# Layer 0's down projection as three rounded products in place of one fp32 product

## The chip, the cores and the metric

The kernel runs on one core of one Trainium2 chip. Times are device microseconds (us) of one execution. A difference of 0.2% (about 1.6 us) is what a measurement of this kernel can tell from no change.

## What is computed

A model of two layers on 1,024 tokens of width 256. Each layer is attention and a feed-forward part (FFN), both with modulated layer norms. The change touches the FFN of layer 0 alone:

```python
h = silu(x @ w_gate) * (x @ w_up)        # [1024, 1024]
g = h.reshape(..., 256, 4)               # quads of neighbouring columns
_, idx = top_k(abs(g), 2)                # the two largest of each four stay
h_sparse = where(kept, g, 0)
x = x + gb * (h_sparse @ w_down)         # [1024, 1024] @ [1024, 256]
```

## The kernel before, in words

Each engine has its own instruction list, written by hand; engines meet only at semaphores. The four parts (`attention0`, `ffn0`, `attention1`, `ffn1`) follow each other with a barrier between them.

`ffn0` works in 8 units: `u = 2 * c + half`, with `c` one of four chunks of 256 tokens and `half` one of two halves of the 1,024 hidden columns. A unit holds `[128, 4, 256]` numbers, 128 quads on the partitions, the four members `e` of a quad side by side, 256 tokens in each.

- **TensorE** runs, for each unit, `wide(u, wg, ...)` (gate product), `down(u - 2)` (down product of the unit two before), `wide(u, wu, ...)` (up product). The exceptions: units 0 and 1 have no down product, the last unit has none between gate and up. After the last up product come `down(5)`, the modulation rows and columns of layer 1 (`mod_rows`, `mod_columns`), `down(6)` and `down(7)`. After units 1 and 3 four transposes (`turn_x`) bring in the next chunk.
- The gate and up products are already split: `product` adds three rounded products (high times high, high times low, low times high) of operands that were split ahead into a rounded value of type `float32r` and the remainder. The down product is one plain fp32 matmul for each `e` and each of two tiles of 128 tokens, and stands in the profile as two matmul records each.
- **ScalarE** takes `silu` of the gate product, then `magnitude` (absolute values of the unit's rows).
- **VectorE** makes `multiply(u)` (into `h[u % 2]`), then `sparsify(u)`: three comparisons, two sums, two further sums (`wins`), and four selections that set what is not kept to zero in `h[u % 2]`. In odd units `add` brings a finished chunk into `x` and `stats` takes its statistics.
- **GpSimd** scales the rows of `w_down` by the gate of layer 0 (8 instructions of 128x256, in place in `staging`), and later makes the low halves of `x`'s turned rows for chunks 2 and 3.

What orders them around the down product: `down(u)` waits for each of the four selections (`sparse`) and, at u = 0, for the eight scaled pieces of `w_down` (`wd_ready`). `multiply(u)` waits for the up product, and for `down(u - 2)`, since it writes the buffer that this one reads.

## Time and profile before

| what | value |
|---|---|
| median of 3 runs | 776.95 us (776.91 to 776.99) |
| span of the profiled execution, first to last instruction | 776.7 us |
| median less span (what lies around the span) | about 0.25 us |
| TensorE busy, whole span | 721.5 us, 93% |
| VectorE busy, whole span | 556.8 us, 72% |
| ScalarE busy, whole span | 447.5 us, 58% |
| GpSimd busy, whole span | 372.5 us, 48% |
| `ffn0`, first matmul to the last `add` | 444.5 to about 531 us |

The profile is one execution; it gives no separate total for itself beside the span. Its engines are called PE (TensorE), DVE (VectorE), ACT (ScalarE) and POOL (GpSimd). Matmuls overlap, so the distance between two starts says what one costs, and not its length. Names are those of the program without buffer numbers: `staging` holds `w_down`, `ff_h` the unit's rows, `ff_y` the down product's sum.

### The profile page before, as it was taken

The numbers are of one execution on the slowest core, as the hardware profiler recorded it, in microseconds if no ns is written. First come the engines' busy times: TensorE is split into PE (matmuls) and PEld (weight loads), VectorE is DVE, ScalarE is ACT, GpSimd is POOL, SyncE is SP. The second block draws the span as 40 slices with busy tenths as digits, with TensorE's granted clock in tenths as the row PEclk, the third lists the DMA queues.
The fourth block names the chain that finished last, engine by engine and source line by source line (L and its number), as shares of the span: only waits on it lengthen the run. The fifth ranks groups of instructions, "written<-read, shape, count | busy, mean of one in ns | idle before, by whom it ended". The sixth has DMA issues, their size and how long they took to land. (4 is left out here: it accounts for less than half of the span.)

```text
span 776.7 us, 12379 instructions
## 1 busy us (share of the span) xinstructions
PE 721.5 (93%) x4376; PEld 620.7 (80%) x4376; DVE 556.8 (72%) x1263; ACT 447.5 (58%) x924; POOL 372.5 (48%) x403
## 2 busy tenths in 40 slices
PE   6979989999999999999999799999979999789997
PEld 4858878888888888888888689997768778577787
DVE  4656786678766787767776788776579788566666
ACT  2756656667566676666655343322578776546432
POOL 2685556635766357653451330002756545205773
PEclk8999999999999999999999999999999999999999
DMA  7000000000000000004000040004100000000001
GB/s 250 14 8 8 8 22 15 14 2 14 22 15 8 8 15 14 14 8 170 7 8 8 9 128 1 1 1 126 39 0 2 1 1 1 0 4 0 1 1 55
DMA packets 19115, 19.85 MB, mean 26 GB/s; under 512 B 2158, under 2 KB 17006, under 8 KB 19054
## 3 DMA queue, kind: packets, MB, share of 16 engines
q1 hardware_dynamic: 17934, 18.40, 7.3%
q8 instruction: 35, 0.57, 0.3%
q10 hardware_dynamic: 1120, 0.66, 0.3%
q14 instruction: 26, 0.21, 0.1%
HBM read 18.01 MB, written 1.05 MB: 25 GB/s over the span
## 5 line engine op out<-in xcount | busy, mean ns | idle before, releaser
L633 ACT ACTIVATE at_probs<-at_probs,at_negmax 128x128 f32<-128x128 f32 (+7 forms) x128 | 99.6, 778 | 31.8 <-DVE at_negmax L736 29.7
L935 POOL TENSOR_TENSOR at_swapped<-at_swapped,at_sin 128x512 f32<-128x512 f32 x40 | 52.1, 1302 | 136.0 <-ACT at_swapped L611 136.0
L736 DVE CUSTOM_DVE_ANT_0 at_probs<-at_scores,causal 128x128 f32<-128x128 f32 (+7 forms) x128 | 96.1, 751 | 16.8 <-PE at_scores L59 16.2
L524 PE MATMUL at_turn<-ident_sb,at_probs 128*128 128x128 f32 x576 | 85.0, 274 | 13.2 <-DVE at_full_T_lo L752 11.1
L524 PEld LDWEIGHTS at_turn<-ident_sb,at_probs 128*128 128x128 f32 x576 | 66.5, 140 | 21.8 <-issue 8.4
L626 ACT ACTIVATE at_edge_T_hi<-at_turn 128x128 fp32r<-128x128 f32 (+3 forms) x128 | 55.5, 434 | 33.2 <-PE at_turn L524 32.8
L57 PE MATMUL at_scores<-at_kT_hi,room 128*128 128x512 f32 (+1 forms) x192 | 66.4, 346 | 3.4 <-DVE at_negmax L736 3.4
L626 ACT ACTIVATE at_full_T_hi<-at_turn 128x512 fp32r<-128x512 f32 x64 | 38.3, 598 | 49.5 <-PE at_turn L524 47.4
L58 PE MATMUL at_scores<-at_kT_lo,room 128*128 128x512 f32 (+1 forms) x192 | 66.7, 347 | 0.0
L59 PE MATMUL at_scores<-at_kT_hi,room 128*128 128x512 f32 (+1 forms) x192 | 66.3, 345 | 0.0
L752 DVE TENSOR_TENSOR at_edge_T_lo<-at_turn,at_edge_T_hi 128x128 fp32r<-128x128 f32 (+3 forms) x128 | 61.3, 479 | 1.1 <-ACT at_edge_T_hi L626 0.8
L939 POOL TENSOR_TENSOR at_plain<-at_plain,at_swapped 128x512 f32<-128x512 f32 x40 | 51.8, 1296 | 5.7
L766 DVE SCALAR_TENSOR_TENSOR x<-at_proj,at_rinv,x 128x256 f32<-128x256 f32 x122 | 52.9, 475 | 0.1
L757 DVE TENSOR_TENSOR at_att_lo<-at_att,at_att_hi 128x512 fp32r<-128x512 f32 x32 | 22.2, 692 | 38.7 <-ACT at_att_hi L640 38.7
L752 DVE TENSOR_TENSOR at_full_T_lo<-at_turn,at_full_T_hi 128x512 fp32r<-128x512 f32 x64 | 44.1, 689 | 6.7 <-ACT at_full_T_hi L626 5.0
L57 PE MATMUL at_proj<-at_wo_hi,at_att_hi 128*128 128x256 f32 x142 | 45.2, 318 | 3.4 <-DVE x L766 1.9
L726 DVE TENSOR_TENSOR at_plain<-at_scores,at_cos 128x512 f32<-128x512 f32 x30 | 20.7, 692 | 32.4 <-ACT at_swapped L611 32.4
L57 PEld LDWEIGHTS at_scores<-at_kT_hi,room 128*128 128x128 f32 x192 | 36.2, 188 | 9.5 <-issue 2.6
L2124 POOL TENSOR_TENSOR ff_fed_lo<-ff_mid,ff_fed_hi 128x512 fp32r<-128x512 f32 x16 | 20.7, 1294 | 47.0 <-ACT ff_fed_hi L1954 47.0
L944 POOL TENSOR_TENSOR room<-at_plain,room 128x512 fp32r<-128x512 f32 x32 | 41.3, 1292 | 2.7
L57 PE MATMUL at_att<-at_edge_T_hi,at_v 128*128 128x512 f32 (+3 forms) x128 | 42.1, 329 | 0.0
L59 PE MATMUL at_att<-at_edge_T_hi,at_v 128*128 128x512 f32 (+3 forms) x128 | 41.4, 323 | 0.0
(405 smaller groups left out, 2292.3 us busy)
## 6 DMA issues: line engine op xcount, KB each, us to landing
at_wq_in<-L_attn_Wqkv SPq DMA_DIRECT2D x16, 128.0 KB, 2.2
at_wo_in<-L_attn_Wo SPq DMA_DIRECT2D x16, 128.0 KB, 2.0
staging<-L_ffn_routed_w SPq DMA_DIRECT2D x7, 256.0 KB, 4.8
ff_wmod<-L_wmod SPq DMA_DIRECT2D x1, 1536.0 KB, 6.2
at_wmod<-L_wmod SPq DMA_DIRECT2D x1, 1024.0 KB, 8.6
staging<-L_ffn_w_gate SPq DMA_DIRECT2D x1, 1024.0 KB, 5.2
staging<-L_ffn_w_up SPq DMA_DIRECT2D x1, 1024.0 KB, 7.3
staging<-L_ffn_w_down SPq DMA_DIRECT2D x1, 1024.0 KB, 9.7
```

Source lines behind the costliest of these rows:

```text
L57: pe.matmul(out, left.hi, right.hi, start=start, stop=False)
L58: pe.matmul(out, left.hi, right.lo, start=False, stop=False)
L59: return pe.matmul(out, left.lo, right.hi, start=False, stop=stop)
L524: mm = pe.transpose(p_turn[t % 2][:, b - b0, :], probs[:, s % 4, b * P:(b + 1) * P], m.ident[:, :])
L626: act.activation(turned_columns(c, b0, b1, i % 4).hi, p_turn[t % 2][:, 0:b1 - b0, :], ACT.Copy)\
L633: act.activation(row, row, ACT.Exp, scale=-1.0, bias=negmax[:, unit % 4:unit % 4 + 1], accum_out=rowsum[:, unit // NT % 2, i:i + 1])\
L736: dve.tensor_tensor_reduce(out=probs[:, s % 4, 0:width], in0=p_scores[s % 2][:, 0:width], in1=m.causal[:, S - width:], scale=-1.0, scalar= ...
L752: dve.tensor_tensor(out.lo, p_turn[t % 2][:, 0:b1 - b0, :], as_f32(out.hi), ALU.subtract).then_inc(turn_lo, 1)
L766: ins = dve.scalar_tensor_tensor(out=rows, in0=bank[:, t * DM:(t + 1) * DM], scalar=rinv[:, head % 2, 2 * j + t:2 * j + t + 1], in1=rows, ...
L935: turning = pool.tensor_tensor(swapped[:, r % 2, :], swapped[:, r % 2, :], sin[:, cols], ALU.mult)
L939: chain.step(pool.tensor_tensor(turned, turned, swapped[:, r % 2, :], ALU.add))
L944: pool.tensor_tensor(out.lo[:, cols], turned, as_f32(out.hi[:, cols]), ALU.subtract).then_inc(rope_done, 1)
```

## The change

The rows of `w_down` and the kept rows of each unit are split into high and low halves, and `down` calls `product` on them.

- `w_down`: after the eight scalings GpSimd makes eight high halves (`tensor_scalar`, 128x256) and then eight low halves (`tensor_tensor`, 128x256, in place in `staging`). `wd_ready` now counts the low halves.
- Kept rows of units 0 to 6: ScalarE copies `h[u % 2]` to `kept_h[u % 2].hi` (`kept_high(u)`, 128x1024), and GpSimd subtracts (`kept_low(u)`, 128x1024). `down(u)` waits for `kept_lo`, once for the whole unit. `kept_high(u - 1)` stands on ScalarE between `silu(u)` and `magnitude(u)`.
- Unit 7: high halves on ScalarE, one for each `e`, after the reads of the modulation rows; low halves on VectorE, one for each `e`, after `sparsify(7)`.
- `multiply(u)` waits for `kept_low(u - 2)` where it waited for `down(u - 2)`.
- The low halves of `x`'s turned rows for chunks 2 and 3 now stand on GpSimd between `kept_low(0)` and `kept_low(1)`, and between `kept_low(2)` and `kept_low(3)`.

```diff
@@ -1013,11 +1013,13 @@
         wg, wu = m.w_gate, pair("wu", [P, KD, I0])
         wu_in = m.staging[:, 2048:4096].rearrange("p (k n) -> p k n", k=KD)
         wd_in = m.staging[:, 4096:6144]
-        wd = wd_in.rearrange("p (c d) -> p c d", d=DM)
+        wd_lo = nc.alloc_sbuf_tensor_at("ff0_wd_lo", [P, I0 // P, DM], F32R, offset=m.staging_at + 4096 * 4)
+        wd = Split(buf("wd_hi", [P, I0 // P, DM], F32R)[:], wd_lo[:, :, :])
         xn = buf("xn", [P, NT, DM])
         h32 = [buf(f"h32{n}", [P, KD, TOKENS]) for n in range(2)]
         sg, absh = buf("sg", [P, 4, TOKENS]), buf("absh", [P, 4, TOKENS])
         h = [buf(f"h{n}", [P, 4, TOKENS]) for n in range(2)]
+        kept_h = [pair(f"kept_h{n}", [P, 4, TOKENS]) for n in range(2)]
         cx, cy, cz = (buf(n, [P, 2, TOKENS], BF16) for n in ("cx", "cy", "cz"))
         sums = buf("sums", [P, 4, TOKENS], BF16)
         wins = buf("wins", [P, 4, TOKENS], BF16)
@@ -1030,6 +1032,7 @@
         gate_mm, up_mm, silu_done, mul_done, abs_done = (sem(n) for n in ("gate_mm", "up_mm", "silu_done", "mul_done", "abs_done"))
         compared, summed, won, sparse = (sem(n) for n in ("compared", "summed", "won", "sparse"))
         down_mm, added = sem("down_mm"), sem("added")
+        kept_hi, kept_lo, last_lo, wd_gated, wd_hi = (sem(n) for n in ("kept_hi", "kept_lo", "last_lo", "wd_gated", "wd_hi"))
         wmod_in, c_wide, mod_mm, mod_read = (sem(n) for n in ("wmod_in", "c_wide", "mod_mm", "mod_read"))
         mods = [p_x[n][:, :, :].rearrange("p k t -> p (k t)") for n in range(2)]
 
@@ -1079,11 +1082,14 @@
                         pe.wait_ge(wd_ready, I0 // P)
                     if c and not half:
                         pe.wait_ge(added, 2 * c)
+                    if u < UNITS - 1:
+                        pe.wait_ge(kept_lo, u + 1)
                     for e in range(4):
-                        pe.wait_ge(sparse, 4 * u + e + 1)
+                        if u == UNITS - 1:
+                            pe.wait_ge(last_lo, e + 1)
                         for n in range(2):
-                            mm = pe.matmul(p_y[n][:, 0:DM], h[u % 2][:, e, n * P:(n + 1) * P], wd[:, 2 * e + half, :],
-                                           start=(half == 0 and e == 0), stop=(half == 1 and e == 3))
+                            mm = product(pe, p_y[n][:, 0:DM], kept_h[u % 2][:, e, n * P:(n + 1) * P], wd[:, 2 * e + half, :],
+                                         half == 0 and e == 0, half == 1 and e == 3)
                     mm.then_inc(down_mm, 1)
 
                 def mod_rows(n):
@@ -1157,6 +1163,18 @@
                         act.wait_ge(compared, 3 * u)
                     act.activation(absh[:, :, :], h[u % 2][:, :, :], ACT.Abs).then_inc(abs_done, 1)
 
+                def kept_high(u):
+
+                    if u >= 2:
+                        act.wait_ge(down_mm, u - 1)
+                    if u < UNITS - 1:
+                        act.wait_ge(sparse, 4 * u + 4)
+                        act.activation(kept_h[u % 2].hi, h[u % 2][:, :, :], ACT.Copy).then_inc(kept_hi, 1)
+                    else:
+                        for e in range(4):
+                            act.wait_ge(sparse, 4 * u + e + 1)
+                            act.activation(kept_h[u % 2].hi[:, e, :], h[u % 2][:, e, :], ACT.Copy).then_inc(kept_hi, 1)
+
                 def read_rows():
                     act.wait_ge(mod_mm, 1)
                     act.activation(m.mod_row[:, 0, :], mods[0][:, 0:DM], ACT.Copy).then_inc(mod_read, 1)
@@ -1180,9 +1198,12 @@
                     silu(u)
                     if u in (2, 4):
                         scale_shift(u // 2 + 1)
+                    if u:
+                        kept_high(u - 1)
                     magnitude(u)
                 read_rows()
                 read_gates()
+                kept_high(UNITS - 1)
 
             @block.vector
             def _(dve):
@@ -1202,7 +1223,7 @@
                     dve.wait_ge(silu_done, u + 1)
                     dve.wait_ge(up_mm, u + 1)
                     if u >= 2:
-                        dve.wait_ge(down_mm, u - 1)
+                        dve.wait_ge(kept_lo, u - 1)
                     dve.tensor_tensor(h[u % 2][:, :, :], sg[:, :, :], p_up[:, :, :], ALU.mult).then_inc(mul_done, 1)
 
                 def sparsify(u):
@@ -1222,6 +1243,13 @@
                     for e, (test, bound) in enumerate(((ALU.is_ge, 2.0), (ALU.is_ge, 1.0), (ALU.is_le, 0.0), (ALU.is_le, 1.0))):
                         kept = h[u % 2][:, e, :]
                         dve.scalar_tensor_tensor(out=kept, in0=wins[:, e, :], scalar=bound, in1=kept, op0=test, op1=ALU.mult).then_inc(sparse, 1)
+
+                def last_low():
+                    u = UNITS - 1
+                    for e in range(4):
+                        dve.wait_ge(kept_hi, u + e + 1)
+                        dve.tensor_tensor(kept_h[u % 2].lo[:, e, :], h[u % 2][:, e, :], as_f32(kept_h[u % 2].hi[:, e, :]), ALU.subtract)\
+                           .then_inc(last_lo, 1)
 
                 def add(c):
                     dve.wait_ge(down_mm, 2 * c + 2)
@@ -1256,6 +1284,7 @@
                     sparsify(u)
                     if u >= 3 and half and u < UNITS - 1:
                         stats(c - 1)
+                last_low()
                 stats(CHUNKS - 2)
                 add(CHUNKS - 1)
                 stats(CHUNKS - 1)
@@ -1269,12 +1298,27 @@
                 pool.wait_ge(wu_ready, KD)
                 for c in range(I0 // P):
                     rows = wd_in[:, c * DM:(c + 1) * DM]
-                    pool.tensor_tensor(rows, rows, m.gate[:, 0, 1, :], ALU.mult).then_inc(wd_ready, 1)
-
-                for c in (2, 3):
-                    pool.wait_ge(hx_hi, c + 1)
-                    pool.tensor_tensor(m.hT.lo[:, :, chunk_cols(c)], h32[c % 2][:, :, :], as_f32(m.hT.hi[:, :, chunk_cols(c)]), ALU.subtract)\
-                        .then_inc(hx_ready, 1)
+                    pool.tensor_tensor(rows, rows, m.gate[:, 0, 1, :], ALU.mult).then_inc(wd_gated, 1)
+                for c in range(I0 // P):
+                    rows = wd_in[:, c * DM:(c + 1) * DM]
+                    pool.wait_ge(wd_gated, c + 1)
+                    pool.tensor_scalar(wd.hi[:, c, :], rows, 1.0, 1.0, ALU.mult, ALU.mult).then_inc(wd_hi, 1)
+                for c in range(I0 // P):
+                    rows = wd_in[:, c * DM:(c + 1) * DM]
+                    pool.wait_ge(wd_hi, c + 1)
+                    pool.tensor_tensor(wd.lo[:, c, :], rows, as_f32(wd.hi[:, c, :]), ALU.subtract).then_inc(wd_ready, 1)
+
+                def kept_low(u):
+                    pool.wait_ge(kept_hi, u + 1)
+                    pool.tensor_tensor(kept_h[u % 2].lo, h[u % 2][:, :, :], as_f32(kept_h[u % 2].hi), ALU.subtract).then_inc(kept_lo, 1)
+
+                for u in range(UNITS - 1):
+                    if u in (1, 3):
+                        c = u // 2 + 2
+                        pool.wait_ge(hx_hi, c + 1)
+                        pool.tensor_tensor(m.hT.lo[:, :, chunk_cols(c)], h32[c % 2][:, :, :], as_f32(m.hT.hi[:, :, chunk_cols(c)]), ALU.subtract)\
+                            .then_inc(hx_ready, 1)
+                    kept_low(u)
 
 
 def attention1(nc, a, m, sems, sb, split):
```

GpSimd's list from the start of `ffn0`, before; `ff_cwide` is for the modulation rows, `staging<-staging,gate` the scaling of `w_down`:

```order
L1263 UNCONDITIONAL_BRANCH [waits barrier_Pool_Activation_PE_DVE_SP_gather]
L1267 TENSOR_SCALAR ff_cwide<-ones,csil 128x128 x2
L1272 TENSOR_TENSOR staging<-staging,gate 128x256 [waits ff0_wu_ready,staged]
L1272 TENSOR_TENSOR staging<-staging,gate 128x256 x7
L1276 TENSOR_TENSOR hT_lo<-ff_h,hT_hi 128x2x256 [waits ff0_hx_hi] x2
L1039 UNCONDITIONAL_BRANCH
```

and now (`ff_wd_hi`, `ff_wd_lo` are the halves of `w_down`, `ff_kept_h_lo` the low half of a unit's kept rows):

```order
L1296 TENSOR_SCALAR ff_cwide<-ones,csil 128x128 x2
L1301 TENSOR_TENSOR staging<-staging,gate 128x256 [waits ff0_wu_ready,staged]
L1301 TENSOR_TENSOR staging<-staging,gate 128x256 x7
L1305 TENSOR_SCALAR ff_wd_hi<-staging 128x256 [waits ff0_wd_gated] x8
L1309 TENSOR_TENSOR ff_wd_lo<-staging,ff_wd_hi 128x256 [waits ff0_wd_hi] x8
L1313 TENSOR_TENSOR ff_kept_h_lo<-ff_h,ff_kept_h_hi 128x1024 [waits ff0_kept_hi]
L1319 TENSOR_TENSOR hT_lo<-ff_h,hT_hi 128x2x256 [waits ff0_hx_hi]
L1313 TENSOR_TENSOR ff_kept_h_lo<-ff_h,ff_kept_h_hi 128x1024 [waits ff0_kept_hi] x2
L1319 TENSOR_TENSOR hT_lo<-ff_h,hT_hi 128x2x256 [waits ff0_hx_hi]
L1313 TENSOR_TENSOR ff_kept_h_lo<-ff_h,ff_kept_h_hi 128x1024 [waits ff0_kept_hi] x4
```

Sixteen instructions now stand between the scaling and the first low half of kept rows, and the low half of chunk 2 (`hT_lo`), once next after the scaling, stands behind that.

ScalarE's list from the first `silu` (`ff0_sg`), before; `ff0_absh` is `magnitude`, `ff0_h320` and `hT_hi` belong to chunk 2:

```order
L1152 ACTIVATE ff0_sg<-ff0_gate 128x1024 [waits ff0_gate_mm]
L1158 ACTIVATE ff0_absh<-ff0_h0 128x1024 [waits ff0_mul_done]
L1152 ACTIVATE ff0_sg<-ff0_gate 128x1024 [waits ff0_mul_done,ff0_gate_mm]
L1158 ACTIVATE ff0_absh<-ff0_h1 128x1024 [waits ff0_compared,ff0_mul_done]
L1152 ACTIVATE ff0_sg<-ff0_gate 128x1024 [waits ff0_mul_done,ff0_gate_mm]
L1142 ACTIVATE ff0_h320<-ff0_x0,modcol 128x256 [waits ff0_hx_ready,ff0_x_mm]
L1142 ACTIVATE ff0_h320<-ff0_x0,modcol 128x256
L1146 ACTIVATE hT_hi<-ff0_h320 128x2x256 [waits ff0_h32_done]
L1158 ACTIVATE ff0_absh<-ff0_h0 128x1024 [waits ff0_compared,ff0_mul_done]
```

and now:

```order
L1158 ACTIVATE ff0_sg<-ff0_gate 128x1024 [waits ff0_gate_mm]
L1164 ACTIVATE ff0_absh<-ff0_h0 128x1024 [waits ff0_mul_done]
L1158 ACTIVATE ff0_sg<-ff0_gate 128x1024 [waits ff0_mul_done,ff0_gate_mm]
L1172 ACTIVATE ff0_kept_h0_hi<-ff0_h0 128x1024 [waits ff0_sparse]
L1164 ACTIVATE ff0_absh<-ff0_h1 128x1024 [waits ff0_compared,ff0_mul_done]
L1158 ACTIVATE ff0_sg<-ff0_gate 128x1024 [waits ff0_mul_done,ff0_gate_mm]
L1148 ACTIVATE ff0_h320<-ff0_x0,modcol 128x256 [waits ff0_hx_ready,ff0_x_mm]
L1148 ACTIVATE ff0_h320<-ff0_x0,modcol 128x256
L1152 ACTIVATE hT_hi<-ff0_h320 128x2x256 [waits ff0_h32_done]
L1172 ACTIVATE ff0_kept_h1_hi<-ff0_h1 128x1024 [waits ff0_sparse]
L1164 ACTIVATE ff0_absh<-ff0_h0 128x1024 [waits ff0_compared,ff0_mul_done]
```

One copy of a unit's kept rows has come in ahead of each `magnitude` from unit 1 on, and waits for `sparsify` of the unit before.

TensorE's list at the first down product, between the last matmul of a gate product and the first of an up product, before (8 fp32 instructions):

```order
L59 MATMUL ff_gate<-hT_hi,room 128x256
L1085 MATMUL ff_y<-staging,ff_h 128x256 [waits ff0_sparse,ff0_wd_ready]
L1085 MATMUL ff_y<-staging,ff_h 128x256
L1085 MATMUL ff_y<-staging,ff_h 128x256 [waits ff0_sparse]
L1085 MATMUL ff_y<-staging,ff_h 128x256
L1085 MATMUL ff_y<-staging,ff_h 128x256 [waits ff0_sparse]
L1085 MATMUL ff_y<-staging,ff_h 128x256
L1085 MATMUL ff_y<-staging,ff_h 128x256 [waits ff0_sparse]
L1085 MATMUL ff_y<-staging,ff_h 128x256
L57 MATMUL ff_up<-hT_hi,ff_wu_hi 128x256 [waits ff0_mul_done]
```

and now, its first rows (24 rounded matmuls in all):

```order
L59 MATMUL ff_gate<-hT_hi,room 128x256
L57 MATMUL ff_y<-ff_wd_hi,ff_kept_h_hi 128x256 [waits ff0_kept_lo,ff0_wd_ready]
L58 MATMUL ff_y<-ff_wd_lo,ff_kept_h_hi 128x256
L59 MATMUL ff_y<-ff_wd_hi,ff_kept_h_lo 128x256
L57 MATMUL ff_y<-ff_wd_hi,ff_kept_h_hi 128x256
L58 MATMUL ff_y<-ff_wd_lo,ff_kept_h_hi 128x256
L59 MATMUL ff_y<-ff_wd_hi,ff_kept_h_lo 128x256
L57 MATMUL ff_y<-ff_wd_hi,ff_kept_h_hi 128x256
```

The four waits for single selections have become one wait for the whole unit's low half and for all of `w_down`'s halves.

## Rows read from the trace of the kernel before

**Rows 1.** `windows`, the whole stretch of the loop: length, busy us (instructions), clock.

```profile
460.00:530.00 70.00, 70.00 (x479) 66.38 (x480) 53.21 (x107) 19.71 (x26) 2.89 (x2) 1.00 0.00 1
```

**Rows 2.** Time line of TensorE: start, length, instructions, idle time ahead.

```profile
466.11 3.62 PE L1085 MATMUL ff_y<-staging,ff_h 128*128 128x256 f32 x16
469.38 0.47 PE L57 MATMUL ff_up<-hT_hi,ff_wu_hi 128*128 128x256 f32 x1
472.37 0.28 PE L57 MATMUL ff_gate<-hT_hi,room 128*128 128x256 f32 x1
475.17 3.62 PE L1085 MATMUL ff_y<-staging,ff_h 128*128 128x256 f32 x16
509.07 0.28 PE L57 MATMUL ff_gate<-hT_hi,room 128*128 128x256 f32 x1
514.67 3.62 PE L1085 MATMUL ff_y<-staging,ff_h 128*128 128x256 f32 x16
518.13 3.62 PE L1098 MATMUL ff_x<-ff_wmod,ff_cwide 128*128 128x256 f32 x16
523.28 7.15 PE L1085 MATMUL ff_y<-staging,ff_h 128*128 128x256 f32 x32
```

**Rows 3.** Time line of VectorE: first unit, and the last unit's product.

```profile
458.69 1.21 DVE L1206 TENSOR_TENSOR ff_h<-ff_sg,ff_up 128x1024 f32<-128x1024 f32 x1
461.03 0.69 DVE L1212 TENSOR_TENSOR ff_cx<-ff_absh 128x512 bf16<-128x512 f32 x1 [1.13 <-ACT ff_absh L1158]
464.55 1.43 DVE L1224 SCALAR_TENSOR_TENSOR ff_h<-ff_wins,ff_h 128x256 f32<-128x256 bf16 x4
465.90 1.22 DVE L1206 TENSOR_TENSOR ff_h<-ff_sg,ff_up 128x1024 f32<-128x1024 f32 x1
518.43 1.22 DVE L1206 TENSOR_TENSOR ff_h<-ff_sg,ff_up 128x1024 f32<-128x1024 f32 x1 [1.79 <-PE ff_y L1085]
```

**Rows 4.** GpSimd: time line, one line's instructions, then groups by shape (mean ns).

```profile
452.04 6.26 POOL L1272 TENSOR_TENSOR staging<-staging,gate 128x256 f32<-128x256 f32 x8 [6.77 <-DVE ff_wu_lo L1244]
L1272 POOL TENSOR_TENSOR staging<-staging,gate x8: 737/751/1268, 452.0 to 457.5; 128x256 f32<-128x256 f32 x8
...
L2130 POOL TENSOR_TENSOR ff_w_lo<-staging,ff_w_hi 128x256 fp32r<-128x256 f32 x8 | 6.0, 744 | 0.7
L2129 POOL TENSOR_SCALAR ff_w_hi<-staging 128x256 fp32r<-128x256 f32 x8 | 3.2, 404 | 0.0
L1741 POOL TENSOR_TENSOR at_wo_lo<-staging,at_wo_hi 128x1024 fp32r<-128x1024 f32 x1 | 2.4, 2410 | 0.1
```

**Rows 5.** ScalarE, groups by shape: copy of 128x1024 from SBUF, rounded.

```profile
L1135 ACT ACTIVATE ff_wu_hi<-staging 128x1024 fp32r<-128x1024 f32 x2 | 2.1, 1052 | 2.2 <-PEq L369 2.2
```

**Rows 6.** Time lines of GpSimd and VectorE where both read SBUF.

```profile
470.77 1.31 POOL L1276 TENSOR_TENSOR hT_lo<-ff_h,hT_hi 128x512 fp32r<-128x512 f32 x1 [12.47 <-ACT hT_hi L1146]
452.72 0.68 DVE L1198 TENSOR_TENSOR hT_lo<-ff_h,hT_hi 128x512 fp32r<-128x512 f32 x1
470.51 0.42 DVE L1217 TENSOR_TENSOR ff_sums<-ff_cx,ff_cy 128x512 bf16<-128x512 bf16 x1
470.96 1.40 DVE L1219 TENSOR_TENSOR ff_wins<-ff_sums,ff_cz 128x512 bf16<-128x512 bf16 x1
```

**Rows 7.** TensorE's idle times and, by `windows`, its clock (after the five counts).

```profile
15.19 1.97 PE L447 MATMUL at_scores<-ident_sb,at_probs 128*128 128x128 f32 x8 [4.02 <-DMA causal<-mask]
14.00:20.00 6.00, 4.82 (x16) 4.16 (x17) 4.58 (x15) 2.22 (x4) 2.26 (x3) 0.50 0.24 77
20.00:21.00 1.00, 1.00 (x5) 0.82 (x4) 0.93 (x4) 0.40 (x1) 0.00 (x0) 0.67 0.00 0
532.32 8.00 PE L66 MATMUL at_idle<-room 128*128 128x512 f32 x27 [1.88 <-PEq L1039]
533.00:536.00 3.00, 3.00 (x9) 2.31 (x8) 2.83 (x11) 0.77 (x2) 0.11 (x1) 0.50 0.25 26
536.00:539.00 3.00, 3.00 (x14) 2.48 (x13) 2.96 (x6) 0.35 (x2) 2.83 (x4) 0.99 0.89 296
```

## The prediction

> **What bounds the kernel now.** I read first where the FFN of layer 0 lies and who works in it. Between 460 and 530 us TensorE is busy for all of the 70 us and at full clock, VectorE for 53.2, ScalarE for 19.7, GpSimd for 2.9 [rows 1]. So from the first units on TensorE sets the time, and a shorter down product can be worth something. The time line of TensorE then gives the price of each piece by the distance of starts [rows 2]: a down product (8 fp32 products) takes 469.38 - 466.11 = 3.27 us; the up product behind it 472.37 - 469.38 = 2.99; a gate product, 24 rounded matmuls of the same shape, 475.17 - 472.37 = 2.80. The 0.19 by which up is longer than gate is paid once behind each fp32 piece. The time line of VectorE shows what feeds the down product [rows 3]: `multiply(0)` starts at 458.69, the last selection ends at 464.55 + 1.43 = 465.98, 7.3 us later, and `down(0)` starts 0.13 behind it. That first one has no slack at all; later ones have a unit's worth, since `down(u - 2)` stands behind the gate product of unit u.
>
> **What the change removes.** Each down product becomes 24 rounded matmuls of the shape of the gate product: 2.80 in place of 3.27, and the 0.19 behind it goes. That is 0.66 a unit for units 2 to 6. At the end `down(5)` gains 0.66 and the last two go from 7.15 [rows 2] to 5.60 plus 0.28, the length of one rounded matmul in the same rows: 1.27. In all 0.66 + 4 x 0.66 + 1.9 = 5.2 us.
>
> The rows give 2.80 against 3.27, 14% less. By the Trainium skill, page "FP8 and Floating Point Precision", section "TensorE Precision Notes", true fp32 takes four passes of the array, which for three products would be a quarter less, 2.45, and not 2.80. The gate product's rows are the same instructions on the same shapes, so I take 2.80; what 2.45 would make stands with the rivals.
>
> **What it adds at the start.** GpSimd ends the scaling of `w_down` at 452.04 + 6.26 = 458.30. Eight high halves at 0.404 and eight low halves at 0.744 follow [rows 4]: 3.2 and 5.95 us, so 461.5 and, alone, 467.45. It is not alone. `sparsify(0)` runs from 461.03 [rows 3] in eleven instructions that read two operands from SBUF, as the low halves do, and the trace shows what two such instructions do to each other [rows 6]: GpSimd's 1.31 us from 470.77 end at 472.08, and VectorE's sum, issued at 470.96, ends at 472.36, 0.28 later, having taken 1.40 in place of about 0.42. The other way round, VectorE's 0.68 at 452.72 goes through at its normal length and one of GpSimd's eight scalings takes 1.268 in place of 0.737 [rows 4], 0.59 of it behind VectorE. So when both have work they alternate, and a pair costs 0.6 + 0.28 for the short VectorE instructions and 0.6 + 0.55 for the three comparisons (0.69 less the 0.14 that a short one saves, 0.42 to 0.28). From 461.5: three pairs of 1.15, to 464.95; five of 0.88, to 469.35, where the halves of `w_down` are done; three selections of 0.36 (1.43 for four [rows 3]), to 470.4, where unit 0 is sparse, 4.4 later than before.
>
> The Trainium skill, page "SBUF — State Buffer", section "Who interferes with whom", says the same of VectorE instructions with two SBUF inputs against any GpSimd instruction that reads SBUF, one blocking the other for its whole length. By its rule `multiply`, with one input in PSUM, is never held, and the comparisons are; the sum above is that of the rows alone.
>
> Then the kept rows of unit 0: ScalarE's copy of 128x1024 costs 1.05 [rows 5], GpSimd's subtraction of 128x1024 costs 2.41 [rows 4], and I add 0.15 for the hand-offs: `down(0)` starts at 474.0 and not at 466.11, **7.9 us late**. Nothing covers this: TensorE's list is fixed, and behind `down(0)` stand the up product of unit 2 and everything else. Low bound: nobody holds anybody, unit 0 is sparse at 465.98, GpSimd is free at 467.45, `down(0)` starts at 469.9, 3.8 late.
>
> **The clock.** TensorE will then stand idle for some 7.6 us. The trace has an idle time of 4.02 us, after which TensorE starts at 15.19 and works at 0.50 of its clock (1.2 GHz) up to about 20.7 (a mean of 0.67 in the microsecond from 20 is two thirds of it at half), and one of 1.88 us before 532.32, with 0.50 until about 536.0 [rows 7]. Work at half clock went on for 5.5 and 3.7 us. I take 4.6, which costs 2.3, since TensorE is what all wait for here. Bounds: 0 (the clock stays), 2.8.
>
> Gate 3 thus starts 7.9 + 2.3 - 0.66 = 9.5 us behind the 472.37 of before.
>
> **The steady units.** A unit lasts 8.4 on TensorE now (9.06 before). A unit's rows pass `multiply` to last selection 7.3, copy 1.05, subtraction 2.41, hand-offs 0.25: 11.0 us from the start of `multiply(u)`. `down(u)` is reached 8.4 + 2.8 = 11.2 after it. It fits by 0.2, so the copies and subtractions of most units cost nothing; their cover is the gate product of the next unit but one. The copy stands ahead of `magnitude` on ScalarE, but `magnitude(u)` waits for `multiply(u)`, 1.22 long [rows 3], which starts when the copy's input is ready too, so that nothing behind it moves. GpSimd's subtraction (1.1 to 3.6 us after the last selection) falls mostly on `multiply` and the wait behind it. In unit 3 the low half of chunk 3 (1.31, as in [rows 6]) stands ahead of the subtraction and holds VectorE once; there the chain is short by about 0.7. At the last up product's end the delay is 9.5 - 4 x 0.66 + 0.7 = 7.6 us.
>
> **The end.** Before, `multiply(7)` waited 1.79 us for `down(5)` [rows 3]; now it waits for `kept_low(5)`, which is long done. TensorE is late by 7.6 - 1.9 = **5.7 us** at the last down product: from 514.67 + 7.6 = 522.3, `down(5)` 2.8, the modulation work 523.28 - 518.13 = 5.15, `down(6)` 2.8, `down(7)` from 533.05. VectorE's chain: `multiply(7)` near 522.5 to 524, selections 7.3 later plus about 1 for a collision with `kept_low(6)`, halves of one quarter about 0.8, so 532 to 533.3. The two tie; the four last steps cost no more than a few tenths.
>
> Sum: 7.9 + 2.3 - 0.66 - 2.64 + 0.7 - 1.9 = +5.7. The span profiled is 776.7, the median 776.95 with about 0.25 around the span, which doesn't change: 782.6 us.
>
> **The rivals.**
> - *The clock stays up.* For it: nothing in the rows, two idle times of less than 7.6 us both ended at half clock. 5.7 - 2.3: 780.3.
> - *The halves of `w_down` and the selections hardly hold each other.* The wait is 3.8, the idle time 3.5, the clock still falls: 3.8 + 2.3 - 0.66 - 2.64 + 0.7 - 1.9 = +1.6: 778.5. Against it stand the rows of both directions.
> - *Faster.* One mechanism, at `down(0)`: the first wait is short enough that the clock holds, and the 5.2 us removed are more than the wait. The wait decides, at about 5.2 without a fall of the clock. At 3.8: -1.4, 775.5. Against it: 1.88 us of idle time was enough for a fall.
> - *The chain of halves binds in every unit.* If each subtraction holds VectorE for 1 us, 11.0 becomes 12.0 and the unit goes back to 9.1: the four gains of 0.66 are lost, the 0.7 is contained: 784.6. For it: the margin is only 0.2. Against: the subtraction falls on an instruction with one operand in PSUM.
> - *Three products cost three quarters of fp32.* 0.35 less for each of eight down products, -2.8, against the rows of the gate product: 779.8.
>
> **Chances and range.** Forecast 0.48 (781 to 784); clock stays 0.13; little collision 0.14; faster or near it 0.07; chain binds 0.14; three quarters 0.02; worse than all 0.02. The range leaves out the fast case, half of the case at 778.5, and what is above 785.2: 778.2 to 785.2. Measurement tells 0.2%, 1.6 us, so "same" is 775.4 to 778.5: faster 0.05, same 0.09, slower 0.86.
>
> **What the next profile would show.** TensorE idle once, at the first `ff_y` matmul, 5 to 8 us, released by GpSimd's `ff_kept_h_lo`; clock 0.50 behind it for 3 to 6 us; GpSimd's eight `ff_wd_lo` longer than 0.744; units of 8.4 to 8.5 us between gate products after that; 24 `ff_y` matmuls 0.117 apart. Wrong would be: `down(0)` before 470, further waits of `ff_y` for `ff_kept_h_lo` in every unit, or the last down product waiting for VectorE by more than half a microsecond.

## The result, and the profile after

The changed kernel takes 783.11 us (median, 782.65 to 784.13); the kernel before, run beside it, takes 776.97 (776.91 to 777.2). The ratio is 1.0072, with a 95% interval of 1.006 to 1.0084: slower by 6.1 us, where the forecast said 5.7. The kernel before was run again beside each later series and had medians of 777.71 to 778.13 there; against the 777.78 of the control below the rise is 5.3 us.

A second run of the unchanged kernel with its trace is used as the control, since its layer 0 FFN begins at almost the same time as that of the changed kernel (443.56 and 443.67 us), so that the two time lines differ by 0.11 us and can be read side by side. Against [rows 2] and [rows 3], 0.88 us is to be added to the times of after. Time lines of TensorE, first the control, then the changed kernel (start, length, instruction, idle time ahead with what ended it; the last row stands behind the layer's end):

```profile
465.12 3.62 PE L1085 MATMUL ff_y<-staging,ff_h 128*128 128x256 f32 x16
...
471.40 0.28 PE L57 MATMUL ff_gate<-hT_hi,room 128*128 128x256 f32 x1
...
513.77 3.62 PE L1085 MATMUL ff_y<-staging,ff_h 128*128 128x256 f32 x16
...
531.41 0.85 PE L66 MATMUL at_idle<-room 128*128 128x512 f32 x2 [1.88 <-PEq L1039]
```

```profile
472.85 0.55 PE L57 MATMUL ff_y<-ff_wd_hi,ff_kept_h_hi 128*128 128x256 f32 x1 [7.36 <-POOL ff_kept_h_lo L1313]
...
475.97 0.38 PE L59 MATMUL ff_y<-ff_wd_hi,ff_kept_h_lo 128*128 128x256 f32 x1
476.19 0.28 PE L57 MATMUL ff_y<-ff_wd_hi,ff_kept_h_hi 128*128 128x256 f32 x1
...
477.25 0.28 PE L57 MATMUL ff_up<-hT_hi,ff_wu_hi 128*128 128x256 f32 x1
480.05 0.28 PE L57 MATMUL ff_gate<-hT_hi,room 128*128 128x256 f32 x1
...
497.40 0.28 PE L57 MATMUL ff_gate<-hT_hi,room 128*128 128x256 f32 x1
500.87 0.39 PE L57 MATMUL ff_y<-ff_wd_hi,ff_kept_h_hi 128*128 128x256 f32 x1 [0.48 <-POOL ff_kept_h_lo L1313]
506.61 0.28 PE L57 MATMUL ff_gate<-hT_hi,room 128*128 128x256 f32 x1
515.18 0.28 PE L57 MATMUL ff_gate<-hT_hi,room 128*128 128x256 f32 x1
520.83 0.27 PE L57 MATMUL ff_y<-ff_wd_hi,ff_kept_h_hi 128*128 128x256 f32 x1
...
536.59 0.69 PE L66 MATMUL at_idle<-room 128*128 128x512 f32 x2 [1.88 <-PEq L1042]
```

The reader is to see one long wait, 7.36 us, ahead of the first down product, released by GpSimd's `kept_low(0)`. From the layer's start to the matmuls behind its end the control has 531.41 - 443.56 = 87.85 us and the changed kernel 536.59 - 443.67 = 92.92: the layer is 5.07 us longer. Everything behind it takes the same time: 775.9 - 531.41 and 781.1 - 536.59 are both 244.5.

What fills that wait is on the time lines of GpSimd, VectorE and ScalarE (answering to [rows 3] and [rows 4]):

```profile
451.19 6.25 POOL L1301 TENSOR_TENSOR staging<-staging,gate 128x256 f32<-128x256 f32 x8 [6.78 <-DVE ff_wu_lo L1272]
457.42 3.07 POOL L1305 TENSOR_SCALAR ff_wd_hi<-staging 128x256 fp32r<-128x256 f32 x8
460.45 7.79 POOL L1309 TENSOR_TENSOR ff_wd_lo<-staging,ff_wd_hi 128x256 fp32r<-128x256 f32 x8
470.36 2.35 POOL L1313 TENSOR_TENSOR ff_kept_h_lo<-ff_h,ff_kept_h_hi 128x1024 fp32r<-128x1024 f32 x1 [2.12 <-ACT ff_kept_h_hi L1172]
```

```profile
460.94 1.22 DVE L1234 TENSOR_TENSOR ff_cy<-ff_absh 128x512 bf16<-128x512 f32 x1
462.09 1.21 DVE L1235 TENSOR_TENSOR ff_cz<-ff_absh 128x512 bf16<-128x512 f32 x1
463.33 0.85 DVE L1237 TENSOR_TENSOR ff_sums<-ff_cx,ff_cy 128x512 bf16<-128x512 bf16 x1
...
466.83 2.36 DVE L1245 SCALAR_TENSOR_TENSOR ff_h<-ff_wins,ff_h 128x256 f32<-128x256 bf16 x4
469.11 1.21 DVE L1227 TENSOR_TENSOR ff_h<-ff_sg,ff_up 128x1024 f32<-128x1024 f32 x1
```

```profile
469.22 1.06 ACT L1172 ACTIVATE ff_kept_h_hi<-ff_h 128x1024 fp32r<-128x1024 f32 x1 [8.09 <-DVE ff_h L1245]
```

Every step follows the one before: scaling, high halves, low halves against the selections, the last selection (469.19), the copy (469.22 to 470.28), the subtraction (470.36 to 472.71), `down(0)` at 472.85. VectorE's comparisons start 1.15 us apart in place of about 0.6 while GpSimd makes low halves, and the four selections take 2.36 and not 1.43 us [rows 3].

The windows of the changed kernel around the wait: stretch, length, then busy time of TensorE, its loads, VectorE, ScalarE and GpSimd, then TensorE's granted clock; the first row answers to [rows 1].

```profile
460.00:530.00 70.00, 62.16 (x502) 61.35 (x501) 58.31 (x102) 26.62 (x33) 27.92 (x19) 0.95 0.00 1
```

```profile
468.00:469.00 1.00, 0.00 (x0) 0.00 (x0) 1.00 (x3) 0.00 (x0) 0.24 (x1) 1.00 0.00 0
469.00:470.00 1.00, 0.00 (x0) 0.00 (x0) 1.00 (x2) 0.78 (x1) 0.00 (x0) 0.67 0.00 0
...
474.00:476.00 2.00, 2.00 (x12) 2.00 (x11) 1.97 (x3) 0.00 (x0) 1.59 (x1) 0.50 0.00 0
476.00:477.00 1.00, 1.00 (x9) 1.00 (x9) 0.96 (x3) 0.00 (x0) 0.00 (x0) 0.91 0.07 16
```

The granted clock fell in the wait, between 469 and 470, and came back just behind 476. The matmuls of `down(0)` start 0.21 us apart (1.2 GHz) up to 475.97 and 0.12 apart from 476.19 on (2.4 GHz), so `down(0)` lasts 477.25 - 472.85 = 4.40 us, and `up(2)` runs at full clock.

### The profile page after: what moved, and what is told of

It is laid out like the page before. It is cut to its first block and busy times, and to the rows that moved or that the text cites. A ratio compares the mean times of both kernels' runs of the same rounds, so it can differ in the third digit from the quotient of the medians.

```text
span 781.1 us, 12551 instructions
## 1 busy us (share of the span) xinstructions
PE 718.4 (92%) x4440; PEld 621.1 (80%) x4440; DVE 565.3 (72%) x1267; ACT 456.9 (58%) x935; POOL 400.8 (51%) x426
```

## The experiments

Each ran in turns with the kernel before on the same chip; a ratio is to that kernel. "Layer" is the length of the layer 0 FFN in the profiled execution, from its first `ff_gate` matmul of line 66 to the first `at_idle` matmul. Medians of different rows come from different series, so rows are compared by their ratios and layers.

| kernel | median us | ratio (95%) | layer us | first down product, us from the layer's start |
|---|---|---|---|---|
| before again (control) | 777.78 | 1.0001 (0.999 to 1.0012) | 87.85 | 21.56 |
| changed | 783.11 | 1.0072 (1.006 to 1.0084) | 92.92 | 29.18 |
| unused halves of `w_down` in before | 780.52 | 1.0037 (1.0024 to 1.005) | 90.57 | 24.15 |
| changed, one fp32 product | 787.06 | 1.0121 (1.0106 to 1.0136) | 97.33 | 29.14 |
| changed, TensorE kept busy | 781.63 | 1.0055 (1.004 to 1.007) | 92.24 | 29.26 |
| changed, high halves of `w_down` on ScalarE | 782.05 | 1.0047 (1.003 to 1.0063) | 90.79 | 27.25 |
| changed, kept halves in two pieces | 780.79 | 1.0044 (1.0031 to 1.0057) | 90.84 | 27.00 |
| two pieces and TensorE kept busy | 778.67 | 1.0009 (1.0 to 1.0018) | 88.79 | 27.59 |
| plain fp32 in units 0 and 1 | 776.56 | 0.9979 (0.9969 to 0.9988) | 86.79 | 21.60 |
| the same with two pieces | 774.27 | 0.9958 (0.9946 to 0.997) | 84.47 | 21.58 |
| plain fp32 in unit 0 alone | 776.33 | 0.9972 (0.996 to 0.9983) | 85.89 | 23.55 |

**The control.** The kernel before, unchanged.

> The kernel before, unchanged, as a control. Both theories: 777.0 us, and a profiled span that lies some 0.25 us under its own time. If the 1.95 us that lie around the changed kernel's span belong to the chip or the day and not to that kernel, they show here too.

777.78 us, ratio 1.0001. Single executions lay between 776.84 and 779.33 us, so the length of the layer in a profile (87.85 here, 87.79 in the profile shown ahead, the two that there are) tells more than a median does. The profiled execution took 777.66 us with a span of 775.9: 1.76 lie around the span and not the 0.25 that was expected.

**Only the collision.** The sixteen halves of `w_down` are made in the kernel before and never read.

> The kernel before with GpSimd's eight high and eight low halves of w_down added, written to buffers that nothing reads, and no wait on them. My theory (GpSimd's subtractions and VectorE's selections hold each other): unit 0 is sparse 3.2 us later, TensorE waits about 3.2 us for it at the first down product, and the time is 780.2, or 781.5 if the clock falls too. Rival (only GpSimd's own list made the changed kernel late): 777.0.

```diff
+                for c in range(I0 // P):
+                    rows = wd_in[:, c * DM:(c + 1) * DM]
+                    pool.wait_ge(wd_ready, c + 1)
+                    pool.tensor_scalar(wd_halves.hi[:, c, :], rows, 1.0, 1.0, ALU.mult, ALU.mult).then_inc(wd_hi, 1)
+                for c in range(I0 // P):
+                    rows = wd_in[:, c * DM:(c + 1) * DM]
+                    pool.wait_ge(wd_hi, c + 1)
+                    pool.tensor_tensor(wd_halves.lo[:, c, :], rows, as_f32(wd_halves.hi[:, c, :]), ALU.subtract)
```

Time lines of GpSimd and TensorE in this run:

```profile
459.88 7.84 POOL L1282 TENSOR_TENSOR ff_wd_lo<-staging,ff_wd_hi 128x256 fp32r<-128x256 f32 x8
```

```profile
467.28 3.69 PE L1087 MATMUL ff_y<-staging,ff_h 128*128 128x256 f32 x16 [2.34 <-DVE ff_h L1226]
```

Nobody waits for these halves, and yet the first down product starts 24.15 - 21.56 = 2.59 us later and the layer is 2.72 longer. It waits for the first of the four selections only, which VectorE reaches late. The expectation had been 3.2 us and not 2.59. VectorE is late although nothing makes it wait for GpSimd: that is the collision, and it alone is worth a third of the first wait.

**Only the product.** All waits and halves stay, but the down product is one fp32 product of the high halves (the terms with low halves are left out).

> The changed kernel with one fp32 product of the two high halves in place of the three rounded ones; all copies, subtractions and waits stay, the low halves are left out of the sum. My theory (rounded products save 0.66 us a unit and 1.9 at the end while TensorE sets the time): 783.1 + 5 x 0.66 + 1.9 - 0.5 for the wait in unit 5 that closes = 787.8, and down product to up product 3.27 us again. Rival (the halves set the pace of the units anyway): under 785.

```diff
-   mm = product(pe, p_y[n][:, 0:DM], kept_h[u % 2][:, e, ...], wd[:, 2 * e + half, :], ...)
+   mm = pe.matmul(p_y[n][:, 0:DM], as_f32(kept_h[u % 2].hi[:, e, ...]), as_f32(wd.hi[:, 2 * e + half, :]), ...)
```

```profile
471.58 5.47 PE L1091 MATMUL ff_y<-ff_wd_hi,ff_kept_h_hi 128*128 128x256 f32 x16 [7.32 <-POOL ff_kept_h_lo L1313]
```

The wait is the same (7.32), the layer is 4.41 us longer than with rounded products, 0.55 for each of eight on average (787.06 us, where 787.8 was expected). The rounded product itself is a gain; it is what feeds it that costs.

**The clock.** 33 matmuls without use are issued ahead of the wait of `down(0)`.

> The changed kernel with 33 matmuls of 128x512 into a free PSUM bank ahead of the first down product's wait, about 7.1 us of work inside the 7.4 us of idle time. My theory (the first wait costs 7.6 us and the clock behind it 1.6): the clock stays at 1.00, the first down product starts where it did, and the time falls by 1.6 to 781.5. Rival (the clock term is not on the path, VectorE sets unit 2): no change, 783.1.

```diff
+                        pe.wait_ge(h32_done, 2)
+                        keep_warm(pe, mods[1], m.room, 33)
                         pe.wait_ge(wd_ready, I0 // P)
```

TensorE's time line in this run, and the window that takes in the start of the first down product:

```profile
464.62 7.69 PE L66 MATMUL ff_x<-room 128*128 128x512 f32 x33
481.50 0.39 PE L57 MATMUL ff_y<-ff_wd_hi,ff_kept_h_hi 128*128 128x256 f32 x1 [0.52 <-POOL ff_kept_h_lo L1315]
...
499.63 0.39 PE L57 MATMUL ff_y<-ff_wd_hi,ff_kept_h_hi 128*128 128x256 f32 x1 [0.55 <-POOL ff_kept_h_lo L1315]
```

```profile
471.00:474.00 3.00, 3.00 (x21) 2.54 (x20) 2.97 (x4) 2.19 (x4) 1.80 (x2) 1.00 0.03 5
```

The clock stays at 1.00, and gate 3 comes 35.02 us after the layer's start and not 36.38: 1.36 gained. At the end only 0.68 of it is left, because the down products of units 1 and 3 now wait 0.52 and 0.55 us for their low halves. In the changed kernel only that of unit 3 had waited (0.48). Either the clock's term is small, or the chain of halves took the rest; the runs with two pieces decide.

**High halves of `w_down` on ScalarE.** They stand between `silu(0)` and `magnitude(0)`, and GpSimd no longer makes them.

> The changed kernel with the eight high halves of w_down made on ScalarE between silu(0) and magnitude(0), where it was idle for 4.5 us; GpSimd goes from the scaling straight to the low halves. My theory: the low halves start 3 us sooner, four of them before the comparisons of unit 0, so unit 0 is sparse about 2 us sooner and the first down product starts 2 us sooner: 781.1, by the same clock. Rival (the first down product waits for something else than this chain): 783.1.

```diff
+                        for c in range(I0 // P):
+                            act.wait_ge(wd_gated, c + 1)
+                            act.activation(wd.hi[:, c, :], wd_in[:, c * DM:(c + 1) * DM], ACT.Copy).then_inc(wd_hi, 1)
```

Time line of TensorE and the window behind `up(1)`:

```profile
460.70 0.39 PE L57 MATMUL ff_up<-hT_hi,ff_wu_hi 128*128 128x256 f32 x1 [1.78 <-DVE ff_h L1234]
472.11 0.55 PE L57 MATMUL ff_y<-ff_wd_hi,ff_kept_h_hi 128*128 128x256 f32 x1 [3.55 <-POOL ff_kept_h_lo L1316]
```

```profile
462.00:465.00 3.00, 3.00 (x16) 3.00 (x15) 2.99 (x3) 0.65 (x1) 3.00 (x4) 0.50 0.00 0
```

The first down product starts 1.93 us sooner and the layer is 2.13 us shorter than in the changed kernel: the place of the high halves on GpSimd was on the path. (The median, 782.05, is 0.95 above the 781.1 expected; the kernel before had 778.13 in this series.) A surprise stands on the first row. `up(1)` had 1.78 us of idle time ahead of it, and the clock was 0.50 from 462 to 465: `up(1)` took 4.46 us in place of 2.91. In the changed kernel the idle time there was 1.42 and the clock stayed up:

```profile
459.18 0.39 PE L57 MATMUL ff_up<-hT_hi,ff_wu_hi 128*128 128x256 f32 x1 [1.42 <-DVE ff_h L1227]
```

```profile
460.00:462.00 2.00, 2.00 (x20) 2.00 (x19) 1.75 (x2) 1.14 (x2) 2.00 (x4) 1.00 0.00 0
```

With the high halves on ScalarE the longer `up(1)` was hidden in the wait for the halves.

**The kept halves in two pieces.** Copy and subtraction take two of the four members at a time, and TensorE waits for each pair.

> The kernel of after, with the halves of the kept rows made in two pieces of two members each (copies on ScalarE, subtractions on GpSimd), and the down product of a member pair waiting only for its own piece. Theory (the chain sparsify, copy, subtract holds TensorE at chunk 0 and holds it again in chunk 3's unit): the first down product starts 1.5 to 2.3 us earlier than in the changed kernel, the wait of 0.48 us ahead of the down product of unit 5 goes, and the layer 0 FFN takes 91 us (it took 92.9): about 1.005 of the kernel before. Rival (only the collisions with VectorE set the first product's time, the subtraction's length is hidden): the layer takes 92.9 as in the changed kernel, 1.007 of before.

```diff
+                        for e in (0, 2):
+                            act.wait_ge(sparse, 4 * u + e + 2)
+                            act.activation(kept_h[u % 2].hi[:, e:e + 2, :], h[u % 2][:, e:e + 2, :], ACT.Copy).then_inc(kept_hi, 1)
...
+                        if u < UNITS - 1 and e % 2 == 0:
+                            pe.wait_ge(kept_lo, 2 * (u - 0) + e // 2 + 1)
```

```profile
470.58 0.55 PE L57 MATMUL ff_y<-ff_wd_hi,ff_kept_h_hi 128*128 128x256 f32 x1 [5.18 <-POOL ff_kept_h_lo L1315]
```

```profile
472.00:474.00 2.00, 2.00 (x11) 2.00 (x11) 1.97 (x5) 1.78 (x4) 0.11 (x1) 0.50 0.00 0
474.00:476.00 2.00, 2.00 (x11) 2.00 (x11) 1.95 (x3) 0.00 (x0) 1.37 (x1) 0.50 0.04 8
```

`down(0)` starts 2.18 us earlier, the wait of 0.48 is gone, the layer takes 90.84 (91 was expected). The clock fell all the same and was back at about the same time, so that 5.26 us lie between the start of `down(0)` and that of `up(2)` where 4.40 did, and `up(2)` itself took 3.02 and not 2.80: the earlier start ran into more work at half clock. (This profiled execution, 781.78 us, is 0.99 above the median; 780.0 - 534.42 = 245.6 us of it lie behind the layer, where the control has 244.5.)

**Both.** The two pieces, and 26 matmuls without use.

> As the run with halves in two pieces, with 26 matmuls of no use issued ahead of the wait of the first down product, so that TensorE does not stand idle there. In the earlier run with such matmuls and undivided halves, only half of the 1.36 us that the clock gave back stayed, because the next down products then waited 0.52 and 0.55 us for their low halves. Theory (the chain took the rest back): with the shorter chain these waits are gone and the layer takes 1.4 to 1.6 us less than in the run with two pieces, about 89.5 us, 1.003 of before. Rival (the clock's term is only 0.7 us whatever the chain does): 90.3 us, 1.004 of before.

```diff
+                        pe.wait_ge(h32_done, 2)
+                        keep_warm(pe, mods[1], m.room, 26)
```

88.79 us: 2.05 less than with two pieces alone, more than the 1.4 to 1.6 expected, and no wait of a down product is left. With one change at a time the clock gave 0.68 and the two pieces 2.08; together they give 4.13, 1.37 more than the sum. The rival that the clock's price was only 0.7 falls. In the kernel with two pieces it was more than the 2.05: `down(0)` and `up(2)` together took 8.28 us there and 5.63 here, 2.65 less, but the unused matmuls lasted until 471.52, though the first low halves were there at 470.88:

```profile
469.59 1.29 POOL L1317 TENSOR_TENSOR ff_kept_h_lo<-ff_h,ff_kept_h_hi 128x512 fp32r<-128x512 f32 x1 [1.02 <-ACT ff_kept_h_hi L1175]
```

So they held the first down product for about half a microsecond (27.59 against 27.00 in the table). In the changed kernel, with less work at half clock, the price is the 1.58 us worked out below.

**The loss avoided.** `down(0)` and `down(1)` stay plain fp32, so that nothing is waited for in chunk 0; `w_down` keeps its fp32 rows. One copy on ScalarE makes its high halves behind `silu(1)`; GpSimd makes the low halves in two groups of four, behind the selections of units 0 and 1.

> Down products of units 0 and 1 stay plain fp32 and wait only for the selections; w_down is scaled in place and kept, its high half is one copy on ScalarE after silu(1), its low half eight subtractions on GpSimd, four behind the selections of unit 0 and four behind those of unit 1; units 2 to 7 use the three rounded products. My theory (the loss sits in the first wait, the gain in the later units): no wait of TensorE at the first down product beyond 0.3 us, clock 1.00, 3 x 0.66 + 1.9 = 3.9 us less than before, at most 0.7 given back in a unit where the chain of halves binds: 773.1 to 773.9. Rival (copies and subtractions slow the steady units by as much as the products save): 776 or more.

```diff
+                def low_weights(u, pieces):
+                    pool.wait_ge(sparse, 4 * u + 4)
+                    pool.wait_ge(wd_hi, 1)
...
+                low_weights(0, range(0, 4))
+                low_x(2)
+                low_weights(1, range(4, 8))
+                kept_low(2)
```

```profile
485.84 0.36 PE L57 MATMUL ff_y<-ff_wd_hi,ff_kept_h_hi 128*128 128x256 f32 x1 [1.28 <-POOL ff_kept_h_lo L1330]
495.10 0.39 PE L57 MATMUL ff_y<-ff_wd_hi,ff_kept_h_hi 128*128 128x256 f32 x1 [0.50 <-POOL ff_kept_h_lo L1330]
```

The layer takes 86.79, 1.06 less than before and not the 3.1 to 3.9 less that was expected. The expectation had allowed 0.7 for the chain of halves. These two rows show 1.78: now that TensorE is not late, the chain from `multiply` to the low half is, in units 2 and 3. The time, 776.56 us, lies where the rival had put it (776 or more), and the rival's mechanism, halves that slow the steady units, is what the two rows show in part.

> The kernel in which units 0 and 1 keep the plain fp32 down product and units 2 to 7 use rounded halves, now with the kept rows' halves in two pieces. In the run with undivided halves the down products of units 2 and 3 waited 1.28 and 0.50 us for their low halves and the time was 0.9979 of before. Theory (these waits are the chain of halves): both are gone, the layer takes 85.0 to 85.5 us (it took 86.8), 0.9955 to 0.996 of before. Rival (the wait is for the sparse rows, late through collisions on the SBUF port): the waits stay over 1 us in sum, the layer takes 86.3 or more, 0.9975 of before.

With the halves in two pieces no down product waits and the layer takes 527.92 - 443.45 = 84.47 us (85.0 to 85.5 was expected), 3.38 less than before: ratio 0.9958 (0.9946 to 0.997), the lowest median of all. The rival, that the rows themselves came late, is out. The layer is 2.3 us shorter than with undivided halves, though the two waits were 1.78 in sum. Nearly all of the rest lies beside the waits: the two gate products ahead of them took 3.05 and 2.99 us net of the wait and take 2.88 and 2.83 here, the two down products 2.94 and 2.97, and 2.88 and 2.87 here. In these rows a wait costs 0.2 to 0.3 us more than its idle time says. The row behind the layer's end:

```profile
527.92 11.61 PE L66 MATMUL at_idle<-room 128*128 128x512 f32 x50 [1.88 <-PEq L1042]
```

**One unit further.** Only `down(0)` stays plain; the halves of `w_down` start with the odd rows, the high ones on ScalarE ahead of `magnitude(0)` and of `magnitude(1)`, three low ones right behind the scaling.

> Only unit 0 keeps the plain fp32 down product; the down weights of odd members are halved first, all high halves on ScalarE, the low halves on GpSimd in three groups placed where VectorE reads one operand from SBUF; the kept rows' halves in two pieces. Theory (the gain of the rounded product is 0.66 us a unit and all of the loss was the halves standing in the way of chunk 0): seven units gain 0.66 each, 4.5 us at most, less the collisions of the low halves with VectorE of up to 1 us: the layer takes 83.5 to 84.5 us, 0.994 to 0.9955 of before. Rival (chunk 1's sparse rows come late as the halves collide with VectorE's chain in it, and down(1) waits 1 to 2 us): 85.5 or more, 0.997 of before.

```diff
...
+                low_weights(0, 1, order[0:3])
+                low_weights(1, 1, order[3:4])
+                low_weights(1, 2, order[4:6])
+                low_x(2)
+                kept_low(1)
+                low_weights(2, 2, order[6:8])
```

```profile
460.75 0.38 PE L57 MATMUL ff_up<-hT_hi,ff_wu_hi 128*128 128x256 f32 x1 [1.75 <-DVE ff_h L1246]
```

```profile
462.00:463.00 1.00, 1.00 (x7) 1.00 (x6) 1.00 (x2) 1.00 (x2) 0.00 (x0) 0.50 0.00 0
463.00:464.00 1.00, 1.00 (x7) 1.00 (x6) 0.96 (x3) 0.65 (x1) 0.00 (x0) 0.50 0.00 0
```

The layer takes 85.89 us, more than the 83.5 to 84.5 expected. The rival's numbers are met (85.5 or more, 0.997), but not its mechanism: no down product waits. What the trace shows was not named in advance: while GpSimd made the first three low halves VectorE's `ff_xn` took longer (3.03 us and not 2.62), `multiply(0)` came 0.4 late, `up(1)` had 1.75 us of idle time ahead, and the clock fell: 4.46 us for an up product of 2.91. The single times lie between 773.62 and 777.23 us and the profile is of the longest. Whether the clock falls there in each of them isn't shown. The mean granted clock of the whole execution was 0.995 or 0.996 in the three shortest (773.62 to 774.55 us) and 0.993 in the other eight, the profiled one among them; that would fit a fall that the three didn't have.

## Why the forecast was right

It was right on the sign and within 0.5 us of the median, and the trace has the terms in the order in which they were put down. Against the control, with the 0.11 us between the two starts taken off:

| term | forecast us | measured us | from |
|---|---|---|---|
| first down product late | 7.9 | 7.62 | 472.85 - 0.11 - 465.12 |
| the clock | 2.3 | 1.58 | (480.05 - 472.85) - (471.40 - 465.12) + 0.66 |
| its own gain | -0.66 | -0.66 | set, to part it from the clock |
| gate 3 late | 9.5 | 8.54 | 480.05 - 0.11 - 471.40 |
| four units to gate 7 | -2.64 + 0.7 | -1.58 | 508.11 in the control, 515.18 - 0.11 |
| the end | -1.9 | -1.89 | 520.83 - 0.11 - 513.77 = 6.95, and 5.07 at the end |
| sum | +5.7 | +5.07 | |

**The first wait.** With 0.88 us added to come to the times of the forecast, the high halves end at 461.4 (forecast 461.5), the low halves at 469.1 (469.35), the last selection at 470.1 (470.4), `down(0)` starts at 473.7 (474.0). The alternation worked out from two collisions in the trace of before [rows 4, 6] gave the length of the whole stretch within 0.3 us. Its rival, little collision, had the first down product 3.8 us late and falls with the 7.62 measured and with the run of the unused halves.

**The clock.** It fell, as forecast, but TensorE worked at half clock for only 3.3 us (472.85 to about 476.2) and not 4.6: 1.6 us. The 4.6 was a mean of two other stretches [rows 7]; taking it over was the one sizeable error, 0.7 us. Such a length doesn't carry over even between two kernels as alike as these: with the halves in two pieces the clock was low over the same stretch (469.5 to 476.3, and 469.4 to 476.2 here), but `down(0)` started at 470.58, and work at half clock went on for 5.7 us. The forecast had taken the length of the work at half clock for a given, and it depended here on when the work began. The rival "the clock stays" is out by the windows.

**The units.** The mechanism was right and the size a little off: the units between gate products lasted 8.57 to 9.21 us (transposes and the wait taken in), where 8.4 to 8.5 had been forecast. The wait of 0.48 us came where the forecast had put one of 0.7: in `down(3)`, whose subtraction stands behind chunk 3's low half. The pieces of the four units took 0.58 us more than the 2.80 assumed for each: a rounded down product measured 2.82 to 2.94, and the gate product ahead of the wait 2.99 net of the wait. Of the 0.58, 0.33 lie in these two pieces beside the wait (3.47 + 2.94 - 0.48 - 5.60). No down product came near 2.45, so the rival of three quarters is out. Why a rounded down product takes 2.82 in one unit and 2.92 in another isn't settled. That the chain has so little slack was right, and two runs show it: with TensorE kept busy it waited 0.52 and 0.55 us, with plain fp32 in units 0 and 1 it waited 1.28 and 0.50, and in both cases the waits went when the chain was cut into pieces.

**The end.** -1.9 was forecast and -1.89 measured. The last low halves ended before TensorE wanted them, in spite of a collision of 1.2 us, that had been put at 1 (the comparison took 1.88 us and not 0.69):

```profile
524.99 1.88 DVE L1233 TENSOR_TENSOR ff_cx<-ff_absh 128x512 bf16<-128x512 f32 x1 [0.38 <-ACT ff_absh L1164]
```

**What was wrong in the reading.** The prediction said that about 0.25 us lie around the span. In every execution of which both were taken the time is 1.7 to 2.1 us above the span (783.07 and 781.1, 777.66 and 775.9). By this the execution profiled before, with a span of 776.7, would be one of some 778.5 us and not one at the median; its own time isn't on record. As the sum was added to the median this moved nothing, but it was said to be tied to the span, and was not. The median rose by 6.14 us (5.33 against the control's median) where the layer grew by 5.07 and all else by 0.1; medians of a few executions that scatter by 1 to 2 us leave such a rest, and that the forecast lies nearer to 6.14 than to 5.07 is chance. Two misses also worked against each other: the clock cost 0.7 less than forecast, and the units gave back 0.4 less.

**The rival of the other side.** It said that the change gains if the first wait ends below some 5 us with the clock kept up. Two runs are consistent with it, though neither tried a short wait in this kernel: with a start 6.03 us late and the clock kept up, the layer is 0.94 us longer than before; with no wait at all it is 3.38 shorter. "1.88 us of idle time was enough for a fall", the argument against it, doesn't carry as far as it was made to: see below.

## What to carry to other kernels

Price a faster product together with the making of its operands at the place where there is no slack, which is the first use: here four steady units gave 1.6 us in all, and the first product, 7.6 us late and run at half clock, cost 9.2. If the path is tight only at the start, leave the first uses in the old form and make the new operands behind them (0.9979 in place of 1.0072, and 0.9958 with the halves in two pieces). When an engine is brought forward, the next chain shows itself at once; cut it into pieces before counting the gain.

## What the runs showed of the hardware

- GpSimd's subtraction of 128x256 from SBUF took 0.744 us elsewhere [rows 4] and 7.79 / 8 = 0.97 us beside `sparsify(0)`, and VectorE's comparisons took 1.21 and not 0.69. With no dependency between the two engines this cost the layer 2.72 us. The Trainium skill, "SBUF — State Buffer", section "Who interferes with whom", says that a VectorE instruction with two SBUF inputs contends with a GpSimd instruction that reads SBUF; the trace agrees. The same page excepts instructions with at most one SBUF input outside the 2-port modes, and `multiply`, with its other input in PSUM, agrees: it took 1.20 us among GpSimd's high halves and 1.22 during `kept_low(1)`.
- An instruction with one tensor input from SBUF did not always go free: `ff_xn`, four normalizations of 128x256, took 3.03 us in place of 2.62 while GpSimd made low halves.
- How long TensorE stood idle did not decide by itself whether its clock fell. Behind 1.75 and 1.78 us ahead of `up(1)` the windows show 0.50, behind 1.42 us in the same place 1.00; ahead of the first down product 3.55, 5.18 and 7.36 us were followed by 0.50. But in the run with unused halves 2.34 us ahead of the first down product left it up:

```profile
465.00:467.00 2.00, 0.00 (x0) 0.00 (x0) 1.97 (x3) 0.00 (x0) 2.00 (x4) 1.00 0.00 0
467.00:468.00 1.00, 0.72 (x3) 0.68 (x4) 1.00 (x3) 0.00 (x0) 0.72 (x1) 1.00 0.00 0
468.00:469.00 1.00, 1.00 (x6) 0.86 (x5) 1.00 (x4) 0.00 (x0) 0.00 (x0) 1.00 0.00 0
```

  What else decides was not tried.
- Ahead of `up(1)`, an idle time longer by 0.33 to 0.36 us was followed by a product 1.55 us longer (4.46 in place of 2.91), at a granted clock of 0.50. The kernels differ in more than this idle time, so that it alone brought the fall isn't shown.
